# One accumulator for the expert sums, with each block's scatters behind the landing of the preceding block's

## The reference

```python
x = x + 0.5 * ffn(layernorm(x))
x = x + attn(layernorm(x))          # decayed linear attention, 16 heads, chunks of 128
x = x + 0.5 * ffn(layernorm(x))     # the same weights

def ffn(x):                         # E = 12 experts, K = 3 for a token, inner width 640
    probs = softmax(x @ Wr + br)
    top_vals, top_idx = top_k(probs, K)
    ew = softmax(top_vals)
    out = 0
    for e in range(E):
        sel = top_idx == e
        w_e = sum(ew where sel) / max(count(sel), 1)         # one weight for an expert
        h = relu(x @ w1[e] + b1[e]) @ w2[e] + b2[e]
        out += any(sel)[..., None] * (w_e * h)
    phi = sigmoid(relu(mean over tokens(out) @ Wp1 + bp1) @ Wp2 + bp2)
    return out * (1 - 0.8 * (phi > 0.7))
```

## Time and profile before

| | us |
|---|---|
| median of 3 runs | 842.14 (838.91 to 844.8) |
| profiled execution | 843.17 |
| its span | 841.3 |
| mean granted clock of PE in the span | 0.914 |
| PE busy | 695.0 (83%) |
| DVE busy | 532.5 (63%) |
| POOL busy | 422.6 (50%) |
| ScalarE busy | 313.9 (37%) |

### The profile page before, as it was taken

How to read it: one execution, slowest core, us unless ns; L and a number is a source line. 1 busy time by engine, 2 the same in 40 slices (tenths; PEclk the granted TensorE clock), 3 DMA queues, 4 the chain that set the end, 5 groups by cost and what they waited for, 6 DMA issues and landing times.

```text
span 841.3 us, 20947 instructions
## 1 busy us (share of the span) xinstructions
PE 695.0 (83%) x6530; PEld 589.0 (70%) x6531; DVE 532.5 (63%) x1085; ACT 313.9 (37%) x704; POOL 422.6 (50%) x302
## 2 busy tenths in 40 slices
PE   1416799999999998659999974179999999999964
PEld 1315687789889997238888863159999999989822
DVE  6895899745555555169899889835555555555505
ACT  3886677433333332022232221243333333333300
POOL 0003488888888885111100100137888888888520
PEclk9757999999999999769999995579999999999977
DMA  9987543656555654710000003043444444444473
GB/s 304 376 312 235 153 70 63 145 99 112 94 112 94 113 94 63 219 50 2 1 0 0 2 1 101 6 133 57 75 75 75 75 75 75 75 75 75 56 211 114
DMA packets 76803, 85.51 MB, mean 102 GB/s; under 512 B 7008, under 2 KB 68448, under 8 KB 76384
## 3 DMA queue, kind: packets, MB, share of 16 engines
q0 software_dynamic: 26880, 36.72, 26.8%
q1 hardware_dynamic: 49888, 48.35, 17.7%
HBM read 50.97 MB, written 34.08 MB: 101 GB/s over the span
## 4 chain that ended last, share of the span: by engine, by line
PE 61%; DVE 11%; issue 10%; DMA 8%; POOL 5%; SPq 3%; ACT 1%; DVEq 0%; ACTq 0%; POOLq 0%
PE PS L796 57%; POOL expert_sums L528 3%; PE PS L853 3%; DMA expert_sums<-zeros 3%; DMA A<-xn_rows,token 2%; DVE A L1335 2%; POOL A L509 2%; DMA W<-w 1%; SPq L432 1%; DMA A<-expert_sums 1%; DVE A L1332 1%; DMA expert_sums<-A,place 1%; DVE A L1539 1%; ACT A L630 1%; DVE A L1246 1%
## 5 line engine op out<-in xcount | busy, mean ns | idle before, releaser
L796 PE MATMUL PS<-A,W 128*128 128x256 f16 (+1 forms) x2356 | 279.1, 277 | 4.0 <-issue 2.2
L796 PE MATMUL PS<-W,A 128*128 (+1 forms) x2228 | 275.2, 280 | 5.6 <-issue 2.4
L509 POOL DMA_INDIRECT A<-xn_rows,token x140 | 177.7, 1270 | 192.7 <-DVE token L1358 123.9
L528 POOL DMA_INDIRECT expert_sums<-A,place x140 | 231.7, 1655 | 64.5 <-issue 40.4
L796 PEld LDWEIGHTS PS<-A,W 128*128 (+1 forms) x2356 | 238.5, 110 | 32.7 <-issue 6.4
L796 PEld LDWEIGHTS PS<-W,A 128*128 128x128 f16 (+1 forms) x2228 | 225.7, 103 | 37.0 <-issue 8.6
L706 ACT ACTIVATE A<-PS,b1s 128x256 f32<-128x256 f32 x340 | 131.5, 478 | 179.2 <-PE PS L796 179.2
L1392 DVE CAST A<-A 128x1280 f16<-128x1280 f32 x68 | 56.5, 831 | 198.0 <-ACT A L706 197.9
L1394 DVE TENSOR_TENSOR A<-A 128x1280 f16<-128x1280 f32 x68 | 101.5, 1493 | 2.3
L796 PE MATMUL PS<-A 32*128 32x128 f32 (+3 forms) x1248 | 66.7, 283 | 31.9 <-DVE A L1335 23.3
L699 ACT ACTIVATE A<-PS 128x512 f16<-128x512 f32 x70 | 41.9, 599 | 114.4 <-PE PS L853 114.3
(11 more groups left out here) (162 smaller groups left out, 430.9 us busy)
## 6 DMA issues: line engine op xcount, KB each, us to landing
W<-w SPq DMA_DIRECT2D x24, 640.0 KB, 11.1
A<-expert_sums SPq DMA_DIRECT2D x16, 512.0 KB, 6.2
expert_sums<-zeros SPq DMA_DIRECT2D x2, 2304.0 KB, 19.0
expert_sums<-zeros SPq DMA_DIRECT2D x12, 384.0 KB, 2.7
xn_rows<-A SPq DMA_DIRECT2D x8, 512.0 KB, 7.1
A<-b SPq DMA_DIRECT2D x2, 1536.0 KB, 8.4
A<-xn_rows,token POOLq DMA_INDIRECT x140
expert_sums<-A,place POOLq DMA_INDIRECT x140
```

Of the source, the lines that this page charges most:

```text
L509: nc.gpsimd.indirect_dma_start(XG[q][:, u * D:(u + 1) * D], None, xn_dram[:, :], bass.IndirectOffsetOnAxis(ap=token[:, at:at + 1], axis=0) ...
L528: nc.gpsimd.indirect_dma_start(sums_dram[f][q][:, :], bass.IndirectOffsetOnAxis(ap=place[:, at:at + 1], axis=0), YO[q][:, u * D:(u + 1) * ...
L796: return nc.tensor.matmul(out_, l, r, start=start, stop=stop_, skip_group_check=True)
```

## The change

There is one accumulator for each call in place of two. A scatter of block b waits until both scatters of block b-1 have landed, where it waited for those of b-2. One clear of 2304 KB stands ahead of call 0's scatters in place of two, and six pieces for call 1 in place of twelve. At a call's end SP waits for both landings and issues four loads in place of eight; PE's column sums have 16 matmuls in place of 32; the four adds of DVE are gone. The pieces of YO (two, by b % 2) and their semaphores stay.

```diff
-        O2 = A[:, bufs_at:bufs_at + T * D].rearrange("p (i d) -> p i d", i=T)
...
-        sums_in = [[sem(f"sums_in{lane}_{c}") for c in range(NC)] for lane in range(LANES)]
+        sums_in = [sem(f"sums_in{c}") for c in range(NC)]
...
-                for lane in range(LANES):
-                    for piece in range(CLEARS):
-                        after_a_block()
-                        clear_sums(1, lane, piece, CLEARS)
+                for piece in range(CLEARS):
+                    after_a_block()
+                    clear_sums(1, piece, CLEARS)
...
-                    for lane in range(LANES):
-                        clear_sums(0, lane, 0, 1)
+                    clear_sums(0, 0, 1)
                     load_between_blocks()
 
                 sp.wait_ge(hl_ready, FREE + NB * (f + 1))
-                for lane, into in ((1, O2), (0, O)):
-                    sp.wait_ge(y_sent[lane], 16 * W * TURNS[lane] * (f + 1))
-                    for c in range(NC):
-                        tiles = slice(c * B, (c + 1) * B)
-                        sp.dma_start(into[:, tiles, :], sums_t[f][lane][:, tiles, :]).then_inc(sums_in[lane][c], 16)
+                for q in range(2):
+                    sp.wait_ge(y_sent[q], 16 * W * TURNS[q] * (f + 1))
+                for c in range(NC):
+                    tiles = slice(c * B, (c + 1) * B)
+                    sp.dma_start(O[:, tiles, :], sums_t[f][:, tiles, :]).then_inc(sums_in[c], 16)
...
                 q = b % 2
-                if b >= 2:
-                    pool.wait_ge(y_sent[q], landed(f, b))
+                if b >= 1:
+                    pool.wait_ge(y_sent[1 - q], landed(f, b - 1))
                     pool.sem_inc(pool_held, 1)
...
                     nc.gpsimd.indirect_dma_start(
-                        sums_dram[f][q][:, :],
+                        sums_dram[f][:, :],
...
             def landed(f, b):
 
-                return 16 * W * (f * TURNS[b % 2] + b // 2)
+                return 16 * W * (f * TURNS[b % 2] + b // 2 + 1)
...
-                pool.wait_ge(sums_cleared[f], 16 * LANES * (1, CLEARS)[f])
+                pool.wait_ge(sums_cleared[f], 16 * (1, CLEARS)[f])
...
-                for lane, sums in ((1, O2), (0, O)):
-                    for c in range(NC):
-                        pe.wait_ge(sums_in[lane][c], 16 * (f + 1))
-                        for b in range(B):
-                            ins = matmul(bank[1][0:B, 0:D], of_batch[:, b, :], sums[:, c * B + b, :],
-                                         lane == 1 and c == 0 and b == 0, lane == 0 and c == NC - 1 and b == B - 1)
-                        ins.then_inc(pool_psum, 1)
+                for c in range(NC):
+                    pe.wait_ge(sums_in[c], 16 * (f + 1))
+                    for b in range(B):
+                        ins = matmul(bank[1][0:B, 0:D], of_batch[:, b, :], O[:, c * B + b, :],
+                                     c == 0 and b == 0, c == NC - 1 and b == B - 1)
+                ins.then_inc(pool_psum, 1)
...
-                Oc = O.rearrange("p (c b) d -> p c (b d)", c=NC)
-                O2c = O2.rearrange("p (c b) d -> p c (b d)", c=NC)
                 for c in range(NC):
-                    for lane in range(LANES):
-                        dve.wait_ge(sums_in[lane][c], 16 * (f + 1))
-                    dve.wait_ge(pool_psum, 2 * NC * f + NC + c + 1)
-                    v.tensor_tensor(Oc[:, c], Oc[:, c], O2c[:, c], ALU.add)
+                    dve.wait_ge(sums_in[c], 16 * (f + 1))
+                dve.wait_ge(pool_psum, f + 1)
                 v.tensor_scalar(pooled_rows[:, :], bank[1][0:B, 0:D], 1.0 / N, None, ALU.mult).then_inc(pool_turned, 1)
```

12 lines of the change are left out of this document (5 added, 7 removed).

## The result

| | before | after |
|---|---|---|
| median (20 runs each) | 843.28 us (838.91 to 845.34) | 839.43 us (835.71 to 842.7) |
| profiled execution | 843.17 | 837.97 |
| its span | 841.3 | 836.2 |
| mean granted clock of PE | 0.914 | 0.937 |
| PE / DVE / POOL busy | 695.0 / 532.5 / 422.6 | 681.8 / 523.0 / 422.1 |

The ratio is 0.995, with an interval of 0.9936 to 0.9965: a gain of 3.9 us that is clear of the noise, where 9.7 were forecast (843.17 to 833.5). In the profiled execution the gain is 5.1 us of span. Split at two points that both traces have, it is 1.63 us up to the transposes of call 0's last block (316.27 before, 314.64 after), 2.05 us from there to call 1's first scatter (253.69 before, 251.64 after, which takes in the end of call 0 and attention), and 1.45 us from that scatter to the end (271.37 before, 269.92 after). Forecast were 5.1, 2.5 and 2.2.

What follows compares the result with a forecast made beforehand. PE was taken to bound the kernel (61% of the chain), held up by POOL at call 0's start and by the calls' ends. 843.17 - 5.1 (clear) - 4.7 (ends), wait 0, gave 833.5 us; range 827 to 840.

Steps and rivals of the forecast that it cites:

- The clear: Start of call 0: the only clear lands 6.5 us earlier, bringing block 13's transposes 5.1 us forward; bounds 2 and 11.5.
- The new wait: Scatter waiting for the block before: 0 us in steady blocks of both calls, because two gathers cover the landing.
- Bounds 0 and 3 us, I take 0: POOL-paced stretch of call 0: a late landing like block 8's could hold POOL 1.2 us in one or two blocks; taken as 0.
- From there POOL keeps its 7.70 per block: Call 0 after scatter 1: POOL's pace stays 7.70 us a block, so everything behind it arrives 5.1 us earlier.
- The forecast of 163.7 for block 13: Call 0: PE starts block 13's transposes at about 163.7 us, where the kernel before had 168.84.
- The 0.30 us of idle time in the steady blocks: Steady blocks: POOL still idles 0.30 us ahead of every scatter and PE's period stays 6.98 us.
- The cycle of 6.55 us: Steady blocks: if the 0.4 us of slack were used up, POOL's cycle would be 6.55 us, below PE's 6.98.
- It decides when the landing comes more than 2.7 us after the issue: PE-paced blocks: threshold in the rival where landings become the cycle, 869 us; chance 0.08.
- The ends: End of each call: last block waits for block 33's landing, but fewer loads and passes and no adds gain 2.5 and 2.2 us.
- the term of 4.7: Gain of 4.7 us from the ends of both calls together; bounds 2 and 7.
- PE taking the lead: Rival, start of call 0: POOL's stretching goes and PE paces from the start; 827 us, chance 0.12.
- The eaten gain: Rival: landing waits or worse POOL pace eat the start's gain, call ends give 1 us each; 839 us, chance 0.19.

Runs made afterwards that it cites:

- no_wait: Changed kernel, but odd blocks scatter into a separate unread table and each scatter waits for the one two blocks before: 825.71 us against 844.05 before.
- no_wait_start: Changed kernel, but call 0's blocks 0 to 9 wait two blocks back, their odd blocks scattering into an unread table: 835.24 us against 843.64 before.
- split_clear: Kernel before, but call 0's two clears count on separate semaphores and only block 1's scatter waits for the second: 836.96 us against 843.64.
- wait_alone: Kernel before, two accumulators and clears kept, but each scatter waits for both scatters of the block before: 846.5 us against 844.05.
- one_clear: Kernel before, but the odd lane's clear for call 0 is issued some 18 us sooner: 840.17 us against 844.05.

## Why the prediction was wrong

The clear gave what was forecast. The new wait, which the sum puts at 0 us but for the last block of each call, costs about 14 us (no_wait): some 4.5 at the start of call 0 and some 7.4 at the two ends.

**The clear: right.** POOL took gather 4 up at 86.73 (86.8 forecast), scatter 0 started at 91.67 (91.5), PE had no gap before block 4. Scatter 1 came at 99.90 (98.9), since the second scatter of block 0 and the gather behind it stood beside DVE's work (2.39 and 2.04 us). Without the new wait and in the even pace (no_wait, no_wait_start, split_clear) block 13's transposes come at 162.3 to 162.8, 6.0 to 6.5 us earlier than before; the forecast was 5.1. This term was right and a little small.

**"Bounds 0 and 3 us, I take 0": the step that failed.** The wait in the stretch that POOL paces was priced as idle time, and as idle time it is small: 0.78 us at block 2 beyond the usual 0.30, and 1.4 at block 9. But its price is the place at which it puts POOL beside DVE. "From there POOL keeps its 7.70 per block" was an average of two paces; the kernel before runs even up to block 4 and alternates after it, and I had the two in view, as the 2.59 of block 8 against 1.58 of block 24, and used them for a rival only. The forecast of 163.7 for block 13 is what the kernels in the even pace reach and better; with the wait at block 2 it is 166.8. The 5.1 us became 2.05 at block 13. The rest of the gap between forecast and trace at the start, 2.05 to 1.63, was lost in steady blocks.

**The 0.30 us of idle time in the steady blocks: right in call 1, wrong in call 0.** In call 1's blocks 9 to 19 the second scatter takes 1.58 us and the period is 6.99, as before. In call 0 the late landing of block 8 put POOL behind the landings, and it stayed there. The cycle of 6.55 us that I gave for that case has one false term, the second scatter's 1.58. What counts is whether it begins ahead of DVE's cast or behind it. DVE and POOL in a steady block of the kernel before, then of the changed one:

```profile
273.20 1.58 POOL L528 DMA_INDIRECT expert_sums<-A,place  x1 [0.30 <-issue]
273.42 0.83 DVE L1392 CAST A<-A 128x1280 f16<-128x1280 f32 x1 [3.23 <-ACT A L706]
...
274.28 1.49 DVE L1394 TENSOR_TENSOR A<-A 128x1280 f16<-128x1280 f32 x1
...
275.08 1.58 POOL L509 DMA_INDIRECT A<-xn_rows,token  x1 [0.30 <-issue]
```

```profile
201.88 0.83 DVE L1386 CAST A<-A 128x1280 f16<-128x1280 f32 x1 [3.40 <-ACT A L701]
202.04 2.11 POOL L523 DMA_INDIRECT expert_sums<-A,place  x1 [0.30 <-issue]
...
204.46 1.02 POOL L504 DMA_INDIRECT A<-xn_rows,token  x1 [0.30 <-issue]
```

Both scatters lie beside the cast. The one that begins 0.22 us ahead of it takes 1.58; the one that begins 0.16 us behind it takes 2.11. So it is in the steady blocks of all traces: some 700 second scatters that begin up to 0.3 us ahead of the cast take 1.57 to 1.59, and 67 that begin 0.07 to 0.45 us behind it take 2.20 down to 1.83, so that they end 2.27 or 2.28 us behind the cast's start, when DVE goes on from the tensor_tensor to its next instruction (275.69 before, 204.16 here). The cover is shorter too: the gather beside the tensor_tensor took 1.58 before and takes 1.02 here, so that the two gathers with their idle times fill 2.9 us in place of 3.5. Behind the landing the second scatter takes 1.75 to 2.6, so that the cycle is 1.61 + 0.30 + 1.96 + 3.13 = 7.0 with the average of the first profile, just PE's 6.98, and 7.4 with the 2.36 us of the second (block 10), above it. "It decides when the landing comes more than 2.7 us after the issue" named the wrong quantity: the landing stayed at 2.0 to 2.3, and the scatter in front of it grew.

In this place the Trainium skill (SBUF — State Buffer, "SBUF: two separate sides" and "Who interferes with whom") bears on it: DVE and GpSimd share a pair of SBUF ports, and by the page GpSimd can't write the descriptors of its DMAs while a DVE instruction holds the pair, which a cast can do, and a tensor_tensor of two SBUF inputs contends with GpSimd's reads. By both sections the one that starts first gets the pair and the other waits. The traces agree as to the cast and as to the order. The page infers that a tensor_tensor does not hold up the writing of descriptors; here the gather that begins inside one takes 1.58 us (275.08) and the one behind it 1.02 (204.46), so for these indirect DMAs that does not hold. The size differs as well: the page lets the later one block in full, which would be up to 0.83 + 1.49 = 2.3 us here, an estimate from the rows of DVE above, and block 2's pair is longer by 1.5 (2.14 + 2.59 against 1.61 + 1.58). No run here takes DVE's instruction away.

**The ends: the mechanism right, the chain too short.** The loads came at 344.78 (344.8 forecast), but I had worked on the times of the kernel before, and the blocks stood 1.63 us earlier by then, so they were 1.6 us late; the passes took 8.61 and 9.83 us (9.3 forecast). I let only the last block wait for a landing. Block 33 waits too: its data were there at 330.6, and it started at 332.91, because block 32's scatters had landed at 332.05. From block 31 on POOL has no gathers left between the scatters, so that nothing covers the landing, and each of these blocks takes landing, wake-up and pair, 6.3 us in this execution (332.91 to 339.18). The pooled rows were scaled 1.81 us earlier in call 0 (361.00 to 357.56, less the 1.63 that came from the start) and 0.91 in call 1 (828.52 to 823.93, less 3.68), so the term of 4.7 measures 2.7. On top came the gate, which takes 2.69 us from there in place of 3.30 in each call; that was in no step, and it is not shown to come from the change (below).

**The range's low side** rested on PE taking the lead. That never came: even in no_wait block 13's transposes start at 162.3, where PE alone would have had them at 157.3.

**The eaten gain**, at 839 us, is what the changed kernel did, in the right places (the POOL-paced stretch and the ends), though at the start not by idle time; it had 0.19. That 839.43 lies inside the range of 827 to 840 is this rival's doing, and not that of the sum.

## What to carry to other kernels

When two engines disturb each other, a wait of under 1 us can cost 4, by moving one engine's work to another place beside the other's: look at where both stand in a block, and price a shift by the worst pair of rows and not by the idle time. A wait that is hidden behind other instructions of its engine is free only where those instructions are; look for the blocks at the end of a loop that no longer have them. And when a resource must be ready before a loop starts, first ask whether each user can wait for its own part: splitting one semaphore brought 6.7 us here, and taking away half the clears, loads, column sums and all the adds brought 3.9.

## What the runs showed of the hardware

- The issue of a scatter on POOL is not one number: 1.54 us in the tail, 1.57 to 1.61 in a steady block when it begins ahead of DVE's cast, 1.73 to 2.59 when it begins behind it. A gather of a steady block is 0.98 to 1.02, and 1.58 when it begins inside the tensor_tensor. In blocks 0 to 8, where DVE is seldom idle, both vary more (scatters 1.57 to 2.59, gathers 0.98 to 2.04).
- A scatter's landing came 2.0 to 2.3 us after its issue ended in nearly all blocks, 3.4 beside a burst of loads, but also 3.3 at call 0's block 1, beside which no burst of loads stands. Why was not tried.
- POOL goes on 0.8 to 0.9 us after the landing for which it waited (332.05 to 332.91; 338.31 to 339.18; each landing is the start of the second scatter and its 3.75 or 3.56 us in the chain of waits).
- PE's clock at the gate was lower in this profile of the kernel before than in that of the changed one. The windows of the gate of call 0 (PE, PEld, DVE, ACT, POOL busy; PEclk, DMA share, GB/s), before and then after:

```profile
361.00:364.30 3.30, 1.89 (x8) 1.63 (x8) 0.58 (x4) 0.54 (x3) 0.00 (x0) 0.62 0.00 0
```

```profile
357.50:360.30 2.80, 1.28 (x8) 1.01 (x8) 0.63 (x3) 0.59 (x3) 0.00 (x0) 1.00 0.00 0
```

The granted clock is 0.62 in the one, partly at the lower of its levels (1.2 and 2.4 GHz), and 1.00 in the other; four small matmuls take 0.61 us in place of 1.02, and the gate of each call is 0.6 us shorter. PE had idled 1.74 us for the last add ahead of the gate before, and 0.62 us after, but that alone does not decide it: wait_alone has the same adds and the same pause, and its granted clock there is 1.00 (361.66 to 364.34):

```profile
362.12 0.28 PE L972 MATMUL PS<-C,A 4*128 4x4 f32 x2 [1.74 <-DVE A L1488]
362.66 0.61 PE L796 MATMUL PS<-pooled,Wp_s 128*128 128x4 f32 x4 [0.26 <-DVE pooled L1490]
```

Of the 13 gates behind adds in all profiles, nine have their four matmuls at 0.61 us; the other four are those of the kernel before and of one_clear. What decides it was not tried, so 1.2 of the 5.1 us between the two profiles are not shown to be the change's.
